# A four-layer graph network on one NeuronCore: packed step rows, node updates by groups of 896 nodes, edge messages summed on VectorE, hinted loops

## What is computed

```python
# 1. attention, 8 heads: k, q, v per node
score = einsum(q[dst], k[src]) * rel_pri / SQRT_DK          # per edge and head
attn  = softmax of score over the edges of one dst
t     = segment_sum(v[src] * attn, dst);  new_h = (t @ Wa + ba) * alpha + h * (1 - alpha)
# 2. four edge layers, ea = silu(edge_attr @ We + be)
agg = segment_sum(relu(x[src] + ea), dst)
y   = x + silu((x + agg) @ W1[l] + b1[l]) @ W2[l] + b2[l];  x = layernorm(y) * gamma[l] + beta[l]
# 3. two graph convolutions: segment_sum of norm * (h @ W)[src] over dst, with self loops, + b, relu
# 4. linear: segment_sum((x[src] @ W), dst) + x @ W_self
```

## Time and profile before

| | |
|---|---|
| median of 3 runs | 10864.15 us (10851.59 to 10875.0) |
| profiled execution, first to last instruction | 10848.8 us |
| PE busy | 5772.8 us (53%), 28701 instructions |
| DVE busy | 3927.8 us (36%), 9234 |
| ACT busy | 1085.3 us (10%), 1937 |
| POOL busy | 6444.5 us (59%), 6594 |
| chain that ended last, by engine | issue 30%, POOL 26%, PE 14%, DVE's sequencer 10%, DVE 9%, DMA 7% |
| mean granted clock of PE | 0.683 |

### The profile page before, as it was taken

The page is one execution under the profiler, slowest core; times in us unless marked ns, Lnnn a source line. Parts: engine busy times, 40 slices in busy tenths (PEclk is TensorE's granted clock), DMA queues, the critical chain, the costliest instruction groups (busy, mean ns, idle before and its releaser), DMA issues.

```text
span 10848.8 us, 178023 instructions
## 1 busy us (share of the span) xinstructions
PE 5772.8 (53%) x28701; PEld 5001.3 (46%) x28702; DVE 3927.8 (36%) x9234; ACT 1085.3 (10%) x1937; POOL 6444.5 (59%) x6594
## 2 busy tenths in 40 slices
PE   3666624444555555555555655555445544454455
PEld 1444424444555545555555545544434444443444
DVE  3445543343333333333333333344322322332223
ACT  1222200000011100111011110111100000000000
POOL 2776512226765377553765547654477777776777
PEclk9677756657777777777777777777655655555567
DMA  4988732113332233222333223322122222222222
GB/s 125 266 263 244 222 88 61 53 48 86 99 86 78 59 105 96 81 78 64 104 93 83 76 71 102 92 74 71 46 53 56 57 54 54 57 59 50 54 55 56
DMA packets 910381, 980.82 MB, mean 90 GB/s; under 512 B 443039, under 2 KB 610361, under 8 KB 907448
## 3 DMA queue, kind: packets, MB, share of 16 engines
q0 software_dynamic: 213248, 462.82, 16.1%
q1 hardware_dynamic: 572380, 399.74, 13.9%
q10 hardware_dynamic: 122332, 98.36, 2.7%
HBM read 801.46 MB, written 165.23 MB: 89 GB/s over the span
## 4 chain that ended last, share of the span: by engine, by line
issue 30%; POOL 26%; PE 14%; DVEq 10%; DVE 9%; DMA 7%; ACTq 1%; SPq 1%; POOLq 0%; ACT 0%
POOL rows L696 25%; PE ps_seg L828 11%; DMA gates_by_edge<-gate 5%; DVEq L376 5%; DVEq L360 2%; DVE sums L1316 2%; DVE onehot L1292 1%; POOL sums L696 1%; ACTq L376 1%; DVEq L332 1%; PE ps_mm L879 1%; PE ps_t L841 1%; DVE gate L1420 0%; DVE msg L1442 0%; DVE h_res L1424 0%
## 5 line engine op out<-in xcount | busy, mean ns | idle before, releaser
L696 POOL DMA_INDIRECT rows<-node_rows,idx x5488 | 5379.1, 980 | 2967.0 <-issue 1594.2
L828 PE MATMUL ps_seg<-msg,onehot 128*128 128x128 f32 (+1 forms) x9880 | 2514.9, 363 | 1832.0 <-DVE sums L1316 1452.4
L1292 DVE SCALAR_TENSOR_TENSOR onehot<-iota_f,win_base,dst_ch 128x512 f32<-128x512 f32 x1984 | 1520.1, 766 | 5114.7 <-issue 2589.2
L828 PEld LDWEIGHTS ps_seg<-msg,onehot 128*128 128x128 f32 x9880 | 2018.9, 261 | 2036.5 <-DVE sums L1316 1305.2
L828 PE MATMUL ps_seg<-rows,onehot 128*128 x5928 | 1395.1, 414 | 1422.7 <-SPq L593 1220.0
L828 PEld LDWEIGHTS ps_seg<-rows,onehot 128*128 128x128 f32 x5928 | 1227.0, 308 | 1585.2 <-issue 1584.7
L828 PE MATMUL ps_seg<-q_res,onehot 128*128 x7904 | 1945.6, 337 | 0.0
L828 PEld LDWEIGHTS ps_seg<-q_res,onehot 128*128 128x128 f32 x7904 | 1617.7, 253 | 0.0
L696 POOL DMA_INDIRECT sums<-kv_rows,idx x784 | 758.8, 968 | 326.6 <-issue 222.5
L717 POOL TENSOR_TENSOR msg<-rows,score 128x512 f32 x247 | 281.6, 1142 | 904.5 <-PE ps_seg L828 684.3
L1442 DVE SCALAR_TENSOR_TENSOR msg<-q_res,rows 128x512 f32 (+1 forms) x992 | 682.4, 688 | 352.5 <-SPq L593 227.7
(11 more groups left out here) (190 smaller groups left out, 2676.3 us busy)
## 6 DMA issues: line engine op xcount, KB each, us to landing
q_res<-gates_by_edge SPq DMA_DIRECT2D x784, 256.0 KB
rows<-node_rows,idx POOLq DMA_INDIRECT x5488
gates_by_edge<-gate ACTq DMA_DIRECT2D x246, 256.0 KB
rows<-dst_padded SPq DMA_DIRECT2D x196, 256.0 KB
value_rows_by_edge<-sums SPq DMA_DIRECT2D x196, 256.0 KB
rows<-value_rows_by_edge SPq DMA_DIRECT2D x196, 256.0 KB, 2.7
idx<-src_padded SPq DMA_DIRECT2D x1568, 2.0 KB
node_rows<-h_res ACTq DMA_DIRECT2D x49, 448.0 KB
```

The source lines that it names most:

```text
L696: pool.indirect_dma_start(target[:, r, j, :], None, table, bass.IndirectOffsetOnAxis(ap=idx[:, r, j:j + 1], axis=0)).then_inc(rows_landed[ ...
L828: last = nc.tensor.matmul(ps_seg[u][:, 0:width], onehot[:, u, j, :], part_(j), start=n_ == 0, stop=n_ == len(terms) - 1)
L1292: V.scalar_tensor_tensor(onehot[:, u, :, :], iota_f[:, :].rearrange("p (a n) -> p a n", a=1).to_broadcast([P, J, P]), win_base[:, ds(w, 1) ...
```

## The change

It has these parts:

- a step's row is one word of packed fields instead of four words; each engine loads 8 words a turn and shifts and masks them;
- node updates go by groups of 7 windows (896 nodes), in one conditional block at the end of a turn on each engine (`update_groups` with its `after`, `attend_group`, `layer_group`, `conv_group`); DVE gives a group's input at the end of one turn and takes its result at the end of the next. The last group is finished behind the loop (`end_last`). In the edge layers and after them ACT has no step loop any more, but a loop over groups. The bias b2 is added by DVE instead of by a product with a row of ones. The two additional steps are gone;
- in the edge layers DVE adds gates and rows and then takes the relu of the sum, two operations, and PE sums `msg` alone, four products a step. Slots are freed by `gates_added`, which is DVE's addition;
- the loops are built for one engine each, with a hint for the back edge (`engine_loop`);
- new buffers `nodes` (input, turned input, hidden values of a group) take the place of small ones, some in space that is free at the time; the group's products use two PSUM banks.

```diff
-    FIELDS = 4
-    CHUNK_, SLOT_, WIN_, END_ = range(FIELDS)
+    CHUNK_, SLOT_, WIN_, GROUP_, END_ = (0, 255), (8, 7), (11, 63), (17, 7), (20, 1)
     UNROLL = 4
-    BEFORE = 3
+    BEFORE = 1
+    ROWS = 2 * UNROLL
...
+        def each_step(eng, name, body, after=None):
+            def load_rows(first):
+                regs = [eng.alloc_register(f"{name}_row{i}_{next(load_no)}") for i in range(ROWS)]
+                eng.load(regs, steps[0:1, ds(first, ROWS)])
+                return [eng.snap(r, donate=True) for r in regs], regs
...
+            with engine_loop(eng, 0, LAST // UNROLL) as i:
+                rows_, regs = load_rows(i * UNROLL)
+                for n in range(UNROLL):
+                    body(i * UNROLL + (n + 1), (n + 1) % 2, i * (UNROLL // 2) + (n + 1) // 2, StepRow(rows_, n + 1 + BEFORE))
+                if after is not None:
+                    after(i * UNROLL + UNROLL, StepRow(rows_, UNROLL + BEFORE))
...
+        def engine_loop(eng, first, end):
+            return nc.Fori(first, end, engines=bass.OrderedEngineSet([eng.engine]), hint_back_edge=True)
...
@@ SP
+                    wait_alone(sp, "sp", segsum_ready, N_STEP * sum_no(k))
...
-                chunk_pass(k, "edges", segsum_ready, N_STEP * sum_no(k), l & 1, also=lambda: layer_loads(l))
+                chunk_pass(k, "edges", gates_added, l * N_ONEHOT, l & 1, also=lambda: layer_loads(l))
+            sp.wait_ge(gates_added, LAYERS * N_ONEHOT)
...
@@ PE
-                terms = [(j, part_) for j in range(J) for part_ in ((rhs,) if also is None else (rhs, also))]
...
+                for j in range(J):
+                    last = nc.tensor.matmul(ps_seg[u][:, 0:width], onehot[:, u, j, :], rhs(j), start=j == 0, stop=j == J - 1)
...
+                def layer_group(s, row):
+                    with pe.If(row.ends(-1)):
+                        g = row.get(GROUP_, GROUPS - 1, -1)
+                        n = l + 1
+                        turn_group(n, g, halves_u)
+                        wait_alone(pe, "pe", layer_weights, (l + 1) * 96)
+                        for h, (a, b) in enumerate(HALVES):
+                            wait_alone(pe, "pe", node_t_ready, (n * GROUPS + g) * 2 + (h + 2))
+                            nc.tensor.matmul(ps_big[h][:, 0:(b - a) * P], w1[:, :], group_t[:, a * P:b * P],
+                                             start=True, stop=True).then_inc(node_mm1_ready, 1)
+                        sum_products(n, g, halves_u, lambda i: [(of_window(group_h, i), w2[:, :])],
+                                     lambda h: wait_alone(pe, "pe", node_h_ready, (l * GROUPS + g) * 2 + (h + 1)))
...
@@ ACT
+                copy_group(l + 1, 0, copies_u)
+                with engine_loop(act, 0, GROUPS - 1) as g:
+                    hidden(g)
+                    store_group(l + 1, g, (l + 1) & 1)
+                    copy_group(l + 1, g + 1, copies_u)
...
@@ DVE
+                def after(s, row):
+                    with dve.If(row.ends(-1 - UNROLL)):
+                        end_group(row.get(GROUP_, GROUPS - 1, -1 - UNROLL))
+                    with dve.If(row.ends(-1)):
+                        g = row.get(GROUP_, GROUPS - 1, -1)
+                        wait_alone(dve, "dve", node_turned, (n * GROUPS + g) * 2 + (g * (halves - 2) + 1))
+                        wait_alone(dve, "dve", agg_added, s + n * N_AGG)
+                        start(g)
...
-                    V.scalar_tensor_tensor(msg[:, u, :, 0:D], gates[:, ds(slot, 1), :, :].rearrange("p s j d -> p (s j) d"),
-                                           -1.0, ring[:, ds(slot, 1), :, :].rearrange("p s j d -> p (s j) d"),
-                                           ALU.mult, ALU.max).then_inc(msg_ready, 1)
+                    V.tensor_tensor(msg[:, u, :, 0:D], gates[:, ds(slot, 1), :, :].rearrange("p s j d -> p (s j) d"),
+                                    ring[:, ds(slot, 1), :, :].rearrange("p s j d -> p (s j) d"), ALU.add)\
+                        .then_inc(gates_added, 1)
+                    dve.wait_ge(gates_added, l * N_ONEHOT + s + 1)
+                    V.tensor_scalar(msg[:, u, :, 0:D], msg[:, u, :, 0:D], 0.0, None, ALU.max).then_inc(msg_ready, 1)
```

More of the change, by code:

```diff
@@ new lines, in sum_products @@
+            def sum_products(n, g, halves, products, ready):
+                wait_alone(pe, "pe", node_finished, n * GROUPS + g + 1)
+                for h, (a, b) in enumerate(HALVES):
+                    ready(h)
+                    for i in range(a, b):
+                        pairs = products(i)
+                        for m, (left, right) in enumerate(pairs):
+                            last = nc.tensor.matmul(ps_mm[h][:, (i - a) * D:(i - a + 1) * D], left, right,
+                                                    start=m == 0, stop=m == len(pairs) - 1)
+                    last.then_inc(node_mm2_ready, 1)
@@ L1035, in _ @@
                     store = store_out
[L1037 to L1040 removed]
+                copies = copies_u if i < 2 else copies_u + copies_self
+                with engine_loop(act, 0, GROUPS - 1) as g:
+                    copy_group(sum_no(k), g, copies)
+                    store(g)
+                copy_group(sum_no(k), GROUPS - 1, copies)
                 store(GROUPS - 1)
```

404 lines of the change are left out of this document (190 added, 214 removed).

## The result

The changed kernel takes 9601.86 us (median of 4 runs, 9595.84 to 9615.88), the kernel before 10861.48 us beside it: a ratio of 0.884, 95% interval 0.8828 to 0.8854. The forecast was 9614 us (9599 for the profiled span, which is 9613.9). The total is right. Three of its terms, for the attention, the edge layers and the score pass, are not, and their errors nearly cancel.

The account below looks back on a forecast made before the run. Bounds: DVE's turn-end waits in the long attention and edge loops; the gather queue in the last three passes. 10848.8 - 45 - 242 - 973 + 10 = 9599 us span, 15 above that 9614; range 9380 to 10110.

Parts of the forecast that it names:

- back edge still missed: Rival for attention and edge layers: the hint fails, DVE still pays 3 us a turn, 10108 us in all; chance 0.12.
- Row load: DVE's load of step rows each turn: from 32 words in 2.11 us to 8 words in 0.6 us.
- Group update: Edge layers: one update of seven windows takes 22 us, six of them 132 us outside the first group.
- Attention, -242 forecast: Attention pass: 61 turns 610 us, group updates 155, both ends 25; 790 us in all, 242 less.
- in this pass PE and its hand-over come to be last: Attention pass: PE and its semaphores, not DVE, set the time, at 2.5 us a step, 10 us a turn.
- Edge layers, -973 forecast: Four edge layers: POOL's gathers last all along; 1070 us three times, then 1105; 4315 instead of 5288 us.
- the gathers' own lengthening: Edge layers: gathers slowed by DVE's new work, 12 us by the estimate, taken as 10 us a layer.
- the 10 us for uneven meeting: Edge layers: 10 us a layer added for uneven meeting, beside 1010 for gathers and 40 between layers.
- relu holds up the gathers: Rival for edge layers: each gather meeting a relu waits for all of it, 9954 us in all; chance 0.15.
- Score pass, -45 forecast: Score pass: ScalarE's row load, 83 us, shrinks from 28 words to 8; half going was put at 45 us.
- the lower bound that I had named: Score pass: a gain of 0, if the DMAs, 0.84 busy, take the room.
- Last three passes, +10 forecast: Convolutions and linear layer: POOL stays last; first interval about 6 us longer, output 9 later; together 10 us more.

Follow-up runs that it names:

- An operand in PSUM: Changed kernel with the one-hot's row of numbers read from a PSUM bank: 9402.72 us, ratio 0.8653 to the kernel before; 0.9235 on the slower kind of chip.
- the old messages: Changed kernel with the kernel before's message (one DVE operation, eight products, slots free after PE's sum): 9514.11 us, ratio 0.8745; 0.9142 on the slower kind of chip.

## Why the prediction was right, and where not

- *What bounds the kernel, and the back edge.* Right: a long body costs DVE 3.15 us a turn, a short one 0.2. I left open whether length or hint removes it; by the runs with and without the hint it is length alone (0.917 and 0.9158). The rival "back edge still missed" failed in its condition, not in its mechanism. The rule named beside it, of the Trainium skill (Runtime: NRT & Kernel Launch, section on instruction fetch mechanics), is that a taken branch whose target isn't held must fetch it first; 2414 packets of instructions before and 43 after agree with that rule. The hint it doesn't name is real, and worth 427 us where bodies are long.
- *Row load.* 0.60 us forecast, 0.602 measured.
- *Group update.* 22 us forecast, 20.4 measured at the end of the first layer, from 3151.85 to 3172.29. Input 1.1 and 1.09; adds and bias 2.5 and 2.5; statistics and scaling 8.7 and 8.7; PE's chain, less what DVE does beside it, 9 and 8.0, as the timeline of DVE has it:

```profile
3151.85 1.09 DVE L1418 TENSOR_TENSOR nodes<-h_res,sums 128x896 f32 x1 [1.08 <-issue]
3160.94 1.15 DVE L1424 TENSOR_TENSOR h_res<-h_res,ps_mm 128x512 f32<-128x512 f32 x2 [8.00 <-PE ps_mm L847]
3162.33 1.09 DVE L1427 TENSOR_TENSOR h_res<-h_res,b_row 128x896 f32<-128x896 f32 x1 [0.24 <-DVE h_res L1424]
3163.57 1.45 DVE L1355 BATCH_NORM_STATS2 group_stats<-h_res 128x6 f32<-128x128 f32 x7
...
3170.36 1.93 DVE L1434 SCALAR_TENSOR_TENSOR h_res<-gate,group_root,b_row 128x128 f32<-128x128 f32 x7
```

- *Attention, -242 forecast, -421 measured.* The failed step is "in this pass PE and its hand-over come to be last": 2.5 us a step at the price of PE's slow products. A turn of four steps has a median of 7.17 us and not 10. PE's products in this pass (min/median/max ns):

```profile
L823 PE MATMUL ps_seg<-msg,onehot x1919: 277/280/597, 1469.7 to 2039.2; 128*128 128x137 f32 x192
```

  They had a median of 435 ns before; the mean granted clock of the pass rose from 0.61 to 0.86, so that most of it ran at the upper level of 2.4 GHz, with PE busy 337 of 611 us where it had been busy 484 of 1032. I took the clock of before for a pass in which PE was to stand idle less. PE's eight products now take 1.20 us a step where the forecast had 2.0. With that alone its 2.5 us a step become 1.7, 6.8 a turn, as an estimate; no run changed the clock by itself. And PE isn't alone last: POOL's multiplication, which had no term in the sum, makes up at least as much of the chain between two group updates (from 1660 to 1700, by line):

```profile
by line: POOL msg L713 38.5%; PE ps_seg L823 34.4%; issue 16.0%; POOLq L713 4.0%; POOLq L324 3.2%; ACT msg L1007 2.9%; ACTq L1007 1.1%; POOLq L375 0.4%
```

  DVE's work isn't in it. POOL's multiplication is also held by the one-hots, as the rows under "An operand in PSUM" show, and the pass was 30 us shorter without that. 61 turns are 437 us instead of 610; the updates and the ends took the other 174 us, where 180 were forecast.
- *Edge layers, -973 forecast, -817 measured.* POOL is last all along, with not one wait in the middle of the first three layers and one of 4 us in the fourth, as forecast. The mis-sized term is the gathers' own lengthening: 12 us a layer over before, measured 827.5 - 775 = 52. The intervals are 44 instead of 40, and the 10 us for uneven meeting did not arise: 1070 + 40 + 4 - 10 is within 6 us of 1110. The last layer has 1138 against 1105: its gathers are the longest (1.065 us), and the interval behind it is 61 us and not 40. By a sign that I had named, a mean of the gathers over 1.05 us, this term had to be called wrong, and it was; the other signs (idle time before the one-hot, gap behind the branch, row load, intervals, clock of 0.56) came out as named, but for the attention.
- *The rival "relu holds up the gathers"*, 85 us a layer more. Its place was right and its price was not: relus hold 0.8 to 2.8 us a layer, since a gather has to start inside one to be held, and only for the rest of it. The larger part, which I took for settled by the small lengthening of before, is the one-hot and the addition. I had quoted the Trainium skill's rule (same section as above) for the fast one-input mode and not its other half, on two inputs from SBUF, which decides here.
- *Score pass, -45 forecast, -5 measured.* More than half of the row load went; the step that failed is that the pass gets shorter by it. The row load fell from 5.9% and 9.8% of the chain to 1.0% and 4.7%, and the stores of the gates, one behind the other, stayed at 38.4% and 69.1% (chain of waits by line, in the stretches of rows 7):

```profile
by line: DMA gates_by_edge<-gate 38.4%; POOL sums L693 36.2%; issue 15.7%; DMA sums<-kv_rows,idx 2.6%; ACTq L955 1.3%; ACTq L368 1.0%; ACT gate L946 0.8%; ACTq L936 0.7%; SPq L536 0.6%; POOLq L324 0.5%; DMA kv_rows<-gate 0.3%; ACTq L324 0.2
...
by line: DMA gates_by_edge<-gate 69.1%; issue 11.2%; ACTq L368 4.7%; ACTq L955 3.5%; PE ps_mm L796 3.0%; ACT gate L946 2.9%; ACTq L936 2.8%; PE ps_big L788 1.1%; ACTq L375 0.7%; ACTq L324 0.6%; ACT attr_t L949 0.5%; ACT L946 0.4%; PE ps_t L
```

  The DMAs were busy 0.84 and are busy 0.85: what the sequencer gave, the DMAs and POOL took. It is the lower bound that I had named. (Half of my 83 us would also be 42 and not 45.)
- *Last three passes, +10 forecast, +21 measured.* By the first gathers of the passes it is +17: the first pass +17, of which 5.6 are its interval (6 forecast) and 11 again held gathers (0.974 instead of 0.960 us), the second -9 (-5 forecast), the third +9 (+9 forecast).
- *Why the total came out.* Attention is 179 us better than forecast, edge layers 156, the score pass 40 and the last three 11 worse, the softmax and the start 13 better. That they cancel is chance. The rest of the change (group updates, packed rows, short loops) carries the whole gain and more: with the old messages in place the ratio is 0.8745.

## What to carry to other kernels

A loop body written out several times can cost much at its back edge (here 3.15 us a turn of DVE in the long loops, 0.2 in the short ones). Look for the gap behind the branch and for packets in the instruction queue, shorten the body first, and hint what stays long. In this kernel, once POOL's gathers were last, each DVE operation that read only SBUF was a tax on them, paid by its place in time and not by its share of the span, and an operand moved to PSUM took the tax away. And the granted clock of a pass is no price for the pass after a change: it went from 0.61 to 0.86 in the attention pass and from 0.75 to 0.56 in the first edge layer.

The one-hot from PSUM with the old messages might join the two gains. It wasn't run.

## What the runs showed of the hardware

- A gather that starts inside a DVE operation with all operands in SBUF, and at least 0.1 us or so behind its start, lasts longer by the rest of that operation less 0.12 us (by some 0.5 us at most, on 0.94). Inside one with an operand in PSUM it doesn't (0.00 us, 619 gathers).
- A multiplication on POOL that starts inside a one-hot has a median of 1.485 us (177 of them) and otherwise 1.058; with an operand of the one-hot in PSUM 1.059 (150).
- On some chips DVE's and SP's register instructions lasted over 0.6 us in 10% and 18% of cases in the edge layers, and the same program took 14 to 15% longer (12494 and 12370 instead of 10860 us). The best kernel of one kind of chip was slower than the changed one on the other (0.9235 against 0.9158), so an edit that frees POOL is only worth what it is where POOL is last.
